# A routed two-expert layer on one core: fewer routing operations, coefficients picked by register, one work item less

## The reference

```python
xn = layernorm(x)
x1 = ifft(fft(xn) * filt).real                  # filt from one scalar of the first 1024 numbers
bits = (sigmoid(x1 @ W_el + b_el) > 0.5)        # 24 bits a token, some of them corrected
s = x1 + corrected @ W_le + b_le
probs = softmax(xn @ router_w.T)                # 8 experts
topk_vals, topk_idx = top_k(probs, 2)
w = topk_vals / (sum(topk_vals) + 1e-6)
ffn = sum over the two experts e of (xn @ expert_weights[e] + probs[e]) * w[e]
out = x + s * silu(ffn)
```

## Time and profile before

| | |
|---|---|
| Median of 3 runs | 1231.86 us (1228.46 to 1235.25) |
| The profiled execution | 1235.18 us, its span 1233.3 us |
| PE busy | 1131.4 us (92%) |
| DVE busy | 1096.8 us (89%) |
| ACT busy | 512.7 us (42%) |
| POOL busy | 877.7 us (71%) |
| DMA packets | 216921, 208.74 MB |

### The profile page before, as it was taken

The page is one execution under the profiler, slowest core; times in us unless marked ns, Lnnn a source line. Parts: engine busy times, 40 slices in busy tenths (PEclk is TensorE's granted clock), DMA queues, the critical chain, the costliest instruction groups (busy, mean ns, idle before and its releaser), DMA issues. The chain is left out here.

```text
span 1233.3 us, 26827 instructions
## 1 busy us (share of the span) xinstructions
PE 1131.4 (92%) x6283; PEld 609.0 (49%) x6284; DVE 1096.8 (89%) x2658; ACT 512.7 (42%) x1151; POOL 877.7 (71%) x857
## 2 busy tenths in 40 slices
PE   5998869725889999999999999999999999999996
PEld 4565545412434455555555555555555555555553
DVE  6899969998877889899989998999999899999985
ACT  4476646664655333333333333333333333333332
POOL 1136655648886588777878887888888788888874
PEclk9999989957999999999999999999999999999999
DMA  8669999403446576666667666666666666666663
GB/s 322 242 212 200 198 149 203 81 23 97 150 144 175 147 172 171 171 174 173 174 166 179 173 173 166 176 174 176 172 169 176 171 175 173 170 178 172 174 167 108
DMA packets 216921, 208.74 MB, mean 169 GB/s; under 512 B 166271, under 2 KB 166271, under 8 KB 212786
## 3 DMA queue, kind: packets, MB, share of 16 engines
q1 hardware_dynamic: 184370, 124.31, 42.8%
q0 software_dynamic: 31360, 79.78, 21.9%
q10 hardware_dynamic: 1152, 4.19, 1.3%
HBM read 123.36 MB, written 47.11 MB: 138 GB/s over the span
## 5 line engine op out<-in xcount | busy, mean ns | idle before, releaser
L1435 PE MATMUL banks<-w_hi,arena 128*128 (+1 forms) x1136 | 432.5, 381 | 6.2 <-DMA arena<-arena 5.9
L1436 PE MATMUL banks<-w_lo,arena 128*128 (+1 forms) x1136 | 432.3, 381 | 0.0
L1437 PE MATMUL banks<-w_hi,arena 128*128 (+1 forms) x1136 | 432.2, 380 | 0.0
L716 ACT ACTIVATE arena<-xbuf,inf 128x512 f16<-128x512 f32 x156 | 112.6, 722 | 532.5 <-DVE xbuf L1225 532.2
L529 POOL DMA_INDIRECT xbuf<-in_L_attn_x,gidx x156 | 189.7, 1216 | 78.9 <-issue 66.2
L531 POOL DMA_INDIRECT inf<-token_info,gidx x156 | 200.2, 1283 | 54.0 <-issue 53.4
L508 POOL DMA_INDIRECT pair_tokens<-tok,slot x112 | 112.6, 1005 | 110.4 <-DVE slot L1058 78.4
L569 POOL TENSOR_TENSOR xbuf<-xbuf 128x512 f32<-128x512 f32 x128 | 162.8, 1272 | 35.8 <-DVE xbuf L1294 28.7
L1435 PEld LDWEIGHTS banks<-w_hi,arena 128*128 128x128 f16 x1136 | 111.4, 98 | 134.3 <-issue 17.1
L1437 PEld LDWEIGHTS banks<-w_hi,arena 128*128 128x128 f16 x1136 | 111.5, 98 | 131.5 <-issue 1.7
L535 POOL DMA_INDIRECT out<-xbuf,sidx x128 | 142.6, 1114 | 40.7 <-issue 40.4
(11 more groups left out here) (305 smaller groups left out, 1728.7 us busy)
## 6 DMA issues: line engine op xcount, KB each, us to landing
xbuf<-in_L_attn_x SPq DMA_DIRECT2D x32, 1024.0 KB, 11.1
arena<-extra_sums SPq DMA_DIRECT2D x128, 256.0 KB
arena<-in_L_ffn_expert_weights SPq DMA_DIRECT2D x8, 1024.0 KB, 11.0
extra_sums<-arena SPq DMA_DIRECT2D x28, 256.0 KB, 2.9
token_info<-info ACTq DMA_DIRECT2D x8, 512.0 KB, 11.5
xbuf<-in_L_attn_x,gidx POOLq DMA_INDIRECT x156
inf<-token_info,gidx POOLq DMA_INDIRECT x156
arena<-arena SPq DMA_TRANSPOSE x128
```

Source lines behind the costliest of these rows:

```text
L716: nc.scalar.activation(hi4[ring(i, k)], uv2[:, b], ACT.Copy, scale=inf2[:, k, 1:2]).then_inc(hi_ready, 1)
L1435: mm(ps, hi[:, c], wh, start=(c == 0), stop=False)
L1436: mm(ps, hi[:, c], wl, start=False, stop=False)
L1437: end = mm(ps, lo[:, c], wh, start=False, stop=(c == C - 1))
```

## The change

1. *Layout of tokens.* Block k of a round is now 512 neighbouring tokens: lane p, step (k, q) holds token i*2048 + k*512 + p*4 + q. A block load is one piece of 1 MB instead of 128 pieces of 8 KB at a pitch of 32 KB; a lane still gets 8 KB in one piece. The store of records is written in pieces of 1 KB instead of 4 KB.
2. *Routing.* The bookkeeping of epsilon, of the factor -0.5 and of the scale goes into neighbouring operations and the constant matrices; eight small VectorE operations a round go. The token numbers are made by a GpSimd iota in `scatter` instead of VectorE.
3. *Turn-over.* The masks for `tokT` are made before the rows are awaited; one product is left after the wait.
4. *Item 0* is dropped; its sum is stored as zeros. The expert order and the places of the low parts are shifted.
5. *Coefficients.* The table `onehot`, its two VectorE operations, one matmul, `main_coef` on GpSimd and the sum on VectorE go. ScalarE reads the two expert numbers of a tile into registers (`value_load`) and scales one column of the record by one column of `unscale` for each. In the extra items the coefficient, too, moves from GpSimd to ScalarE.
6. Two of the four rings of parts lie in another buffer.

```diff
-    EXPERT_ORDER = (*range(1, NE), 0)
-    LOW_AT = {1: 4, 2: 5, 3: 6, 9: 7}
+    EXPERT_ORDER = (*range(2, NE), 1, 0)
+    LOW_AT = {1: 4, 2: 5, 3: 6, 12: 7}
-    x_tiles = x_rows.rearrange("(i p t) e -> p i t e", p=P, t=TB)
+    x_tiles = x_rows.rearrange("(i k p q) e -> p i k q e", p=P, k=U, q=GT)
-    info_tiles = info_dram.rearrange("(i p t) w -> p i t w", p=P, t=TB)
+    info_tiles = info_dram.rearrange("(i k p q) w -> p i k (q w)", p=P, k=U, q=GT)
...
-                sp.dma_start(xbuf[:, k], x_tiles[:, i, k * GT:(k + 1) * GT, :]).then_inc(ld_x[k], 16)
+                sp.dma_start(xbuf[:, k], x_tiles[:, i, k]).then_inc(ld_x[k], 16)
...
             def scatter(i, buf):
+                after(pool, scattered[buf], 16 * TB * (i // 2))
+                token_ids(i, buf)
+                pool.wait_ge(iota_ready, i + 2)
                 pool.wait_ge(slot_ready, i + 1)
...
-            def main_coef(i, k):
-                m = (i - XR) * U + k
-                pool.wait_ge(ld_x2[k], 32 * (i + 1))
-                if not (first_main(i) and k < 2):
-                    pool.wait_ge(coef_sum, m - 1)
-                G.tensor_tensor(ctmp[:, k % 2], onehot[:, bass.ds(m, 1)].rearrange("p o s e -> p (o s) e"),
-                                inf2[:, k, 8:8 + NE].unsqueeze(1).broadcast_to([P, 2, NE]), ALU.mult).then_inc(coef_mul, 1)
...
+            def extra_coef(n):
+                k, c = n % U, 8 + PATH[n][1]
+                act.wait_ge(ld_x2[k], landed(n // U, k))
+                after(act, x_scaled, n - U + 1)
+                nc.scalar.activation(cab[:, k, 0:1], inf2[:, k, c:c + 1], ACT.Copy, scale=tq[:, 7, n:n + 1]).then_inc(coef_ready, 1)
+            def main_coef(i, k):
+                m = (i - XR) * U + k
+                act.wait_ge(ld_x2[k], landed(i, k))
+                if first_main(i):
+                    act.wait_ge(x_scaled, NX - U + k + 1)
+                else:
+                    act.wait_ge(z_ready, m - U + 1)
+                for c in range(2):
+                    e = act.value_load(tile_exp[0:1, c, bass.ds(m, 1)], min_val=0, max_val=NE - 1)
+                    nc.scalar.activation(cab[:, k, c:c + 1], inf2[:, k, bass.ds(e + 8, 1)], ACT.Copy,
+                                         scale=unscale[:, bass.ds(e, 1)]).then_inc(coef_picked, 1)
...
                 if not (last and k + 2 >= U):
                     bits_part(*at(i, k, 2))
+                    main_coef(*at(i, k, 2))
...
-                def factor():
-                    dve.wait_ge(newton, 4 * i + 3)
-                    V.tensor_scalar(rt, rt, -0.5, 1.5, ALU.mult, ALU.add).then_inc(newton, 1)
...
-                lk(V.tensor_tensor(eq, lg, each(m1, NE), ALU.is_equal), beside[1])
+                lk(V.tensor_tensor(dl, lg, each(m1, NE), ALU.subtract), beside[1])
-                lk(V.tensor_tensor(sc, eq, along(ramp_h[:, :], NE), ALU.mult), beside[2])
+                lk(V.scalar_tensor_tensor(sc, dl, 0.0, along(ramp_h[:, :], NE), ALU.is_equal, ALU.mult), beside[2])
-                V.tensor_tensor(dl, lg, each(m1, NE), ALU.subtract)
-                lk(V.tensor_reduce(m2, over(l2), AXX, ALU.max), beside[6])
-                V.tensor_tensor(d2, m2, m1, ALU.subtract).then_inc(dx_ready, 1)
+                V.tensor_reduce(d2, over(l2), AXX, ALU.max).then_inc(dx_ready, 1)
...
-            link(V.tensor_copy(tokTf[:, :, :], tokT[:, :, :]))
-            V.scalar_tensor_tensor(tokTf[:, 0], iota_c, tend[:, 0:1], tokTf[:, 0], ALU.is_lt, ALU.mult)
-            link(V.scalar_tensor_tensor(tokTf[:, 1], iota_c, tsel[:, 1, 2:3], tokTf[:, 1], ALU.is_lt, ALU.mult))
-            V.scalar_tensor_tensor(tokTf[:, 1], iota_c, tsel[:, 1, 1:2], tokTf[:, 1], ALU.is_ge, ALU.mult).then_inc(rows_float, 1)
+            V.tensor_tensor(tokTf[:, :, :], tokT[:, :, :], tokTf[:, :, :], ALU.mult)
+            dve.wait_ge(last_mm, 1)
+            V.tensor_copy(tokTl, psum[:, 0, 0:P]).then_inc(rows_float, 1)
...
-            for n in range(NX):
+            for n in range(1, NX):
                 extra_step(n)
                 if n in LOW_AT:
                     low_parts(LOW_AT[n])
                 if n == NX // 2:
-                    marks_alike()
-                if n == NX // 2 + 4:
-                    marks_scaled()
+                    experts_of_tiles()
```

208 lines of the change are left out of this document (96 added, 112 removed).

## The result

| | kernel before | changed kernel |
|---|---|---|
| median of 4 runs each, same chip, us | 1233.55 | 1251.88 |
| lowest, highest | 1228.46, 1237.16 | 1242.06, 1256.80 |
| ratio, 95% interval | | 1.0155, 1.0110 to 1.0201 |
| profiled execution, us | 1235.18 | 1247.85 |

The account below looks back on a forecast made before the run. Limits by stage: VectorE and DMA in routing, GpSimd in quiet extra items, TensorE in main items. Savings 2.6 + 0 + 1.0 + 3.0 + 3.6 + 5.0 + 1.0 = 16.2 us from median 1231.9 gave 1216, range 1200 to 1227.

Parts of the forecast that it names:

- Routing operations: Routing pass: eight fewer VectorE operations save 0.8 us a round, counted only before DMA fills and after the last block: -2.6.
- Block loads: Routing pass: contiguous loads of x change only addresses; scatters that slow everything stay, so 0 us taken.
- first rival: Routing pass: blocks come faster beside scatters, waiting goes and middle rounds gain, 14.6 us together: 1201; chance 0.27.
- Record stores: Routing pass: smaller store pieces cost 0, hidden because nobody waits until a round later; upper end +10 us.
- the savings drown: Small record pieces lengthen DMA-bound rounds by 2 us each, and extra items gain only 1 of 5.0: 1225 to 1230; chance 0.15.
- Turn-over: After the last scatter matmul: only a copy is left of VectorE's 1.45 us, masks cost 0.2 earlier: 1.0 us saved.
- Item 0: Start of the extra items, bound by VectorE: one item less saves 2.7 to 3.6 us; 3.0 taken.
- Mark table: Extra items: two VectorE operations of 2.27 us that hold up the chain go; bounds 0 and 5.0, 3.6 us taken.
- Coefficients of extra items: Extra items: GpSimd sheds the coefficient, TensorE limits next, 0.3 us an item gained, ScalarE's operation hidden: 5.0 us saved.
- Main coefficients: Main items: ScalarE's register loads and operations, 1.2 us a coefficient, delay nothing; bounds 0 and 11, 1.0 us gain taken.
- third rival: Main loop: ScalarE becomes the bound if a coefficient costs over 1.5 us, adding 38 us: 1254; chance 0.06.

Follow-up runs that it names:

- fixed_three: Changed kernel with the old token layout, the extra items' coefficient at the head of ScalarE's step, and two record buffers: 1216.6 us, ratio 0.9885.
- both: Changed kernel with two record buffers and the extra items' coefficient at the head of ScalarE's step: 1211.4 us, ratio 0.9875.
- store_four: Kernel before, with a round's records stored in four DMAs, in pieces of 1 KB instead of 4 KB: 1223.2 us, ratio 0.9997.
- pool_coef: Changed kernel with the old token layout and GpSimd making the extra items' coefficients ahead of its gather: 1219.9 us, ratio 0.9918.
- kernel before with copies: Kernel before, with 28 added 128 KB copies of x within HBM ahead of block loads in the routing pass: 1224.7 us, ratio 1.0001.
- fixed_two: Changed kernel with the old token layout and the extra items' coefficient at the head of ScalarE's step: 1207.4 us, ratio 0.9872.
- first comparison: Unmodified changed kernel against the kernel before, four runs each, no added DMA traffic: 1251.9 us, ratio 1.0155.
- coef_first: Changed kernel with the extra items' coefficient moved from behind the high part to the head of ScalarE's step: 1225.1 us, ratio 0.9931.
- its two repairs with copies: Changed kernel with added HBM copies and either the old token layout (1233.2 us, 1.0062) or two record buffers (1229.2 us, 1.0057); unrepaired 1246.5 us, 1.0160.

## Why the prediction was wrong

By the profiled executions the forecast sum was -16.2 and the measured one +12.7. Of the 28.9 between them, 19.9 are in the extra items (-8.6 forecast, +11.3 measured), 7.7 in the routing pass, 1.6 in the start of the items. Two steps failed: what was called hidden in the extra items' coefficients, and what was called hidden in the record store.

- **Routing operations** (-2.6): right. Undisturbed rounds went from 26.25 to 25.5, and in executions without late blocks this came in the rounds that I had counted at nothing, too: 146.2 us against 149.4 in six rounds, -3.2.
- **Block loads** (0): right. The blocks still land in 4.9 us without scatters and in 7 to 31 us beside them. The first rival (1201) is false: the old layout is nowhere measurably slower than the contiguous one, not even where two record buffers take the stores out of the comparison (fixed_three 0.9885, both 0.9875). The rule in the Trainium skill ("DMA: Bandwidth & Descriptors", section "Latency and other measured facts"), that laying tiles out contiguously restores the rate lost at large powers of two, finds no loss to restore at a pitch of 32 KB, which lies under the smallest that it lists (512 KB): 1.0036 with the old layout, 1.0030 with the new.
- **Record stores** (0, upper end +10): the step failed. I wrote "What hides it is only that nobody waits for the store until a round later" and left it there. A round later is 22 to 26 us, and a store of the kernel before already took up to 18.3 us. In the new layout it took 29.6, past the cover, and ScalarE, which waits for it, holds x. The executions bear this out together: the latest store landed after 27.8 us or more in six of the seven profiles with contiguous blocks and 1 KB pieces, and after 18.4 us at most in the eight with 4 KB pieces. The rival "the savings drown" had the small pieces in it, but as 2 us of transfer a round and not as a wait of ScalarE. Whether the size of the pieces or the new order of the blocks beside them makes the store late is open; store_four, the one run that parts them, came when nothing was late.
- **Turn-over** (-1.0 and 1.0 of routing operations): right, -2.4 for -2.0, and -1.8 in quiet runs (31.4 against 33.2).
- **Item 0** (-3.0): right in sign. -2.3 in the kernels with a good place for the coefficient (38.6 against 40.9); the late coefficient eats it.
- **Mark table** (-3.6): too small. pool_coef has GpSimd's coefficients and no mark table, and its items stretch is 78.5 us against 84.8 to 87.0, so 6 to 9 us. I had said of the 5.73 us gather that the change does not touch it; in every kernel without the table no gather of x or record in the extra items passes 3.4 us. In the kernel before VectorE, late by the table's operations, runs from 351.21 to 358.39 without a pause, and the gather from 353.57 to 359.30 lies beside it. store_four and the kernel before with copies repeat it: a gather of 5.74 us, ending 0.9 us after such a run of VectorE in all three. The Trainium skill ("SBUF — State Buffer", section "SBUF: two separate sides") says that GpSimd and VectorE share a port pair under an exclusive lock, which VectorE's operations with two SBUF inputs take only against a GpSimd operation that reads SBUF. The operations beside the gather have two SBUF inputs and the gather reads its row numbers (`gidx`) from SBUF, so the rows fit it; no run here isolates it.
- **Coefficients of extra items** (-5.0): the step that failed most. I checked that ScalarE had time for the operation (0.28 us, 23.8 of 34 us busy) and wrote "hidden". I did not ask what stands ahead of it in ScalarE's order and who waits for its result. What stands ahead is a wait for the landing of a gather; who waits is GpSimd's next gather but one. That costs 14 to 20 us of items against the right place (94.2 and 79.8, 92.6 and 76.8, 96.0 and 76.0). And the gain itself, with the right place, is hardly to be seen: 78.5 us with GpSimd's coefficients, 76.0 to 80.3 in the four kernels with ScalarE's early ones. By item the next limit stood closer than I took it: pool_coef's last 22 items took 3.27 us each with the same three operations and still no gap on GpSimd, and the four kernels without the coefficient there 3.15 to 3.25, not 3.07. What sets those 3.15 to 3.25 was not looked into.
- **Main coefficients** (-1.0): the gain is not confirmed (820.0 to 824.5 us without the table, 819.3 to 821.1 with it). The cost was taken too high: a register load took 0.279 us (median) instead of 0.73, and two coefficients took ScalarE 0.85 us (800.63 to 801.48 us in one item) instead of 2.4. ScalarE did not become the bound, so the third rival is false.

With both mistakes undone (fixed_two and fixed_three also take back the new layout) the change is worth 1.2 to 1.3%: 1233.6 x 0.9872 = 1217.8. That this is near the forecast of 1216 is luck: it is made up otherwise, with more from rounds and mark table and less from the coefficients.

**Open**: why transfers are slow in some executions and on some chips (kernel before: 1223.7 to 1233.6 us from set to set), and whether the copies had a part in it. That the first comparison's surplus over 1.0030 is the store wait is shown by its profile, and for the same wait in other sets by coef_first against both and by the changed kernel against its two repairs with copies; no repair ran beside the first comparison itself.

## What to carry to other kernels

An instruction that moves to an engine with time to spare must be placed by its result's consumer: read what the instructions ahead of it wait for, and follow the chain until it either ends or comes back to itself; a loop over n items costs its length divided by n on each. When a transfer is called hidden, put its longest landing in the trace beside the time until its buffer is written again, not its mean share of the queue. And measure such a change in a second set of runs, with the kernel before and the changed kernel in each, since a cover that just suffices shows itself only when the queues are slow. An engine without a gap (GpSimd here) tells that it may be the bound, not how far off the next one is.

## What the runs showed of the hardware

- The first record store of 512 KB (issued at 83 to 85 us, ahead of most scatters) landed in 5.6 to 6.7 us in pieces of 1 KB and in 2.8 to 3.5 in pieces of 4 KB. It was not alone: the DMA share from 83 to 90 us was 0.69 in the changed kernel. Stores of 1 KB pieces after the last block, too, landed in 2.9 to 3.1 us in some executions.
- Register loads from an SBUF table took 0.272/0.279/1.055 us (min/median/max of 256) on ScalarE's queue, less than on TensorE's (0.344 median) or SyncE's (0.728).
- In three kernels a gather of GpSimd, 1.37 us at the median, took 5.73 to 5.74 us beside a run of VectorE operations without a pause, and ended 0.90 to 0.91 us after it (kernel before, store_four, kernel before with copies).
- Late transfers need not cost anything: with block landings of up to 22.8 us and stores of up to 14.4 us beside the 28 copies, the kernel before stood at 1.0001 to itself without copies.
